# Output projection, cross-attention and feed-forward of a decoder layer merged into one program

## What is computed

```python
x = x + attn(layernorm(x), Wq, Wk, Wv, Wo)      # ends with ctx @ Wo.T
x = x + xattn(layernorm(x), ctx, ctx)           # 8 heads of 64 token rows per sequence
x = x + ffn(layernorm(x), w_gate, w_up, w_down)

def xattn(q, k, v):                             # q is the normed x, rows are tokens
    qh = q.reshape(b * 8, 64, 512); kh = k.reshape(b * 8, 64, 512); vh = v.reshape(b * 8, 64, 512)
    sm = softmax(einsum('bdm,bdn->bmn', qh, kh) / 8, axis=-1)
    return einsum('bmn,bcn->bcm', sm, vh).reshape(b, 512, 512)

def qlinear(x, w):                              # the feed-forward's three products
    wq, ws = round_clip(w / mean|w|); xq, xs = round_clip(x / (max|x| / 127))
    return (xq @ wq.T) * xs * ws
ffn = qlinear(silu(qlinear(x, w_gate)) * qlinear(x, w_up), w_down)
```

## Time and profile before

| | |
|---|---|
| median of three runs | 911.53 us (908.85 to 912.01) |
| the profiled execution | 906.05 us |
| its span, first to last instruction | 904.2 us |
| busy share of the span, PE / DVE / ACT / POOL | 87% / 77% / 50% / 45% |
| TensorE's mean granted clock | 0.958 of full speed |
| a and b, up to the last DVE instruction of b | 0 to 403.2 us |
| c, first transpose to last norm | 409.3 to 481.3 us |
| d, first to last compute | 487.6 to 713.2 us |
| e, from its first load to the end | 713.6 to 904.2 us |

### The profile page before, as it was taken

The page is one execution under the profiler, slowest core; times in us unless marked ns, Lnnn a source line. Parts: engine busy times, 40 slices in busy tenths (PEclk is TensorE's granted clock), DMA queues, the critical chain, the costliest instruction groups (busy, mean ns, idle before and its releaser), DMA issues. The chain is left out here.

```text
span 904.2 us, 14319 instructions
## 1 busy us (share of the span) xinstructions
PE 789.2 (87%) x4306; PEld 404.1 (45%) x4306; DVE 696.3 (77%) x1982; ACT 453.7 (50%) x791; POOL 410.4 (45%) x412
## 2 busy tenths in 40 slices
PE   2999589999999999977884899999998379999997
PEld 1888334444444444436662444434433034444443
DVE  7554489888888889814775899898986478989984
ACT  2566147666776767652222555445544134455442
POOL 1556399999940000001223576667666323433331
PEclk9999779999999999998996899999999789999999
DMA  7987545555523223116995555655552224445443
GB/s 265 345 285 250 184 130 169 153 168 147 145 58 85 71 72 81 40 32 217 315 326 192 146 152 158 177 154 158 159 165 80 72 51 94 106 113 112 126 99 94
DMA packets 137101, 134.46 MB, mean 149 GB/s; under 512 B 87232, under 2 KB 99136, under 8 KB 133952
## 3 DMA queue, kind: packets, MB, share of 16 engines
q1 hardware_dynamic: 111488, 104.18, 39.6%
q10 hardware_dynamic: 23808, 16.78, 6.6%
q0 software_dynamic: 1728, 12.58, 4.2%
HBM read 89.65 MB, written 33.03 MB: 136 GB/s over the span
## 5 line engine op out<-in xcount | busy, mean ns | idle before, releaser
L584 DVE CUSTOM_DVE_ANT_0 b_junk<-b_p,mask_qk 128x128 bf16<-128x128 f32 (+3 forms) x512 | 217.7, 483 | 34.6 <-PE b_p L609 34.3
L531 ACT ACTIVATE b_probs<-b_p 128x512 f32<-128x512 f32 (+1 forms) x352 | 176.7, 560 | 49.0 <-PE b_p L641 27.2
L609 PE MATMUL b_p<-b_ks,b_qs 96*128 96x128 bf16 (+3 forms) x512 | 127.5, 314 | 16.0 <-DMA b_ks<-k_parts 10.0
L971 ACT ACTIVATE d_probs<-d_p 128x512 f32<-128x512 f32 x128 | 74.3, 594 | 106.5 <-PE d_p L1077 106.5
L638 PE MATMUL b_p<-b_qs,b_ks 98*128 98x512 bf16 (+1 forms) x352 | 123.0, 364 | 2.8 <-DMA b_qs<-b_mrow 1.8
L944 POOL TENSOR_TENSOR d_halves<-d_probs 128x1024 f32<-128x1024 f32 x32 | 76.2, 2382 | 54.0 <-ACT d_probs L971 53.9
L730 POOL TENSOR_SCALAR c_veps<-c_mv 128x1 f32<-128x1 f32 x16 | 7.1, 446 | 204.2 <-DVE c_mv L779 204.2
L995 DVE TENSOR_REDUCE d_mx<-d_p 128x1 f32<-128x512 f32 x128 | 83.7, 670 | 18.6 <-PE d_p L1060 17.5
L1341 PE MATMUL e_pg<-wg,e_xt 128*128 128x512 bf16 x256 | 67.0, 385 | 18.7 <-DMA e_xt<-e_xq 18.7
L609 PEld LDWEIGHTS b_p<-b_ks,b_qs 96*128 96x128 bf16 x512 | 45.3, 100 | 81.5 <-DVE b_mx L584 19.5
L1060 PE MATMUL d_p<-d_kk,qh 128*128 128x512 f32 x128 | 62.3, 493 | 21.6 <-DVE d_kk L1010 12.4
(11 more groups left out here) (141 smaller groups left out, 1512.0 us busy)
## 6 DMA issues: line engine op xcount, KB each, us to landing
k<-in_ctx SPq DMA_DIRECT2D x64, 128.0 KB, 2.6
qh<-x_normed_high SPq DMA_DIRECT2D x64, 128.0 KB, 2.8
q_parts<-a_parts SPq DMA_DIRECT2D x16, 384.0 KB, 4.3
b_qs<-q_parts SPq DMA_DIRECT2D x32, 192.0 KB, 3.4
a_x<-in_x SPq DMA_DIRECT2D x4, 1024.0 KB, 5.6
a_wst<-in_w_gate SPq DMA_DIRECT2D x4, 1024.0 KB, 6.8
a_wst<-in_w_up SPq DMA_DIRECT2D x4, 1024.0 KB, 8.5
a_wst<-in_w_down SPq DMA_DIRECT2D x4, 1024.0 KB, 8.5
```

Source lines behind the costliest of these rows:

```text
L531: nc.scalar.activation(pblock(j % 2, kb)[:, j0:j0 + nj, c:c + w], p2[(NE * j + n) % BANKS2][:, 0:nj * w].rearrange("p (j c) -> p j c", j=n ...
L584: best = nc.vector.tensor_tensor_reduce(out=junk[:, 2 * ((NU * i + k) % BANKS1) + n, 0:w], in0=bank[:, c:c + w], in1=keep["mask_qk"][:, SE ...
L609: last = nc.tensor.matmul(p1_bank(i, k)[:, c:c + w], qs[0:STACK, s, j, qt * P:(qt + 1) * P], ks[0:STACK, s, 0:w], start=True, stop=True)
L971: nc.scalar.activation(probs[:, s3, n, :], p2[(KD * s3 + n) % BANKS][:], ACT.Exp, scale=SCALE).then_inc(exps, 1)
```

## The change

The last three programs become one, `rest_of_layer` (names r_ in the trace), in one block, after the same a and b. What it does:

- Self-attention writes its output straight into an SBUF tile `tok` (16 tiles of 128 tokens), instead of a staging tile that ACT's queue stored to DRAM. The output projection reads `tok`, adds x and writes back to `tok`; cross-attention adds to it; the feed-forward reads it. The DRAM tensors `attn_out`, `x1` and `x2` and their loads and stores are gone. The normed rows still go through DRAM.
- `in_turn` puts the three stages' steps into one order for every engine: the first four steps of cross-attention (0 to 3) stand behind the last four of the output projection; the feed-forward's steps 0 and 1 behind cross-attention's 31 and 33, and its steps 2 to 9 behind cross-attention's 35 to 42.
- The reciprocal is taken on the 16 by 64 distinct sums of a pair: ACT copies `pd` to `den`, ACT's queue brings one row of each head into `few` (two DMAs), DVE inverts it, SP's queue stores it to DRAM (one DMA) and loads it back spread over 64 partitions each (two DMAs, `rden`). ACT copies `pn` to `y`, and DVE multiplies `y` by `rden`, both in SBUF.
- PE does F and S of a step without a break, then `sum_probs` and two parts of `weigh` in even steps, the other two in odd ones, and each lags the scores by more steps.
- In the feed-forward's steps SP's queue turns `zq` (before: `xq`) ahead of `hq`, no longer behind it.

The core of the diff:

```diff
-                if 0 <= j4 < STEPS:
-                    s, g = j4 % BATCH, j4 // BATCH
-                    act.wait_ge(p1_used, USE[i, OUT] + 1)
-                    act.dma_start(scr["o"][SEQ * s:SEQ * (s + 1), bass.ds(HEADROWS * g, HEADROWS)].rearrange("(t p) c -> p t c", p=P),
-                                  o[:, s, :, :]).then_inc(o_out[s], 16)
...
-                        nc.vector.tensor_tensor(o[:, j % UNROLL, :, :].rearrange("p t (j d) -> p t j d", j=GSZ), turned[:, :, :, 0:HDIM],
+                        s, g = j % BATCH, j // BATCH
+                        nc.vector.tensor_tensor(tok[:, TPB * s:TPB * (s + 1), HEADROWS * g:HEADROWS * (g + 1)].rearrange("p t (j d) -> p t j d", j=GSZ), turned[:, :, :, 0:HDIM],
...
+        C_LAST, D_LAST, E_LAST = TILES + 3, HEADS_X + 11, TILES + 5
+        D_EARLY = 4
+        E_BESIDE = {HEADS_X - 1: 0, HEADS_X + 1: 1}
+        E_BESIDE.update({HEADS_X + 3 + k: 2 + k for k in range(D_LAST - HEADS_X - 3)})
+
+        def in_turn(attend_output, attend_context, feed):
+
+            for i in range(C_LAST):
+                attend_output(i)
+                if i >= C_LAST - D_EARLY:
+                    attend_context(i - (C_LAST - D_EARLY))
+            for i in range(D_EARLY, D_LAST):
+                attend_context(i)
+                if i in E_BESIDE:
+                    feed(E_BESIDE[i])
+            for i in range(len(E_BESIDE), E_LAST):
+                feed(i)
...
+        def pair_due(i, behind):
+
+            s = i - behind
+            return s // 2 if s >= 0 and s % 2 == 0 and s < HEADS_X else None
 
...
+                p = pair_due(i, 10)
+                if p is not None:
+                    sp.wait_ge(inv_done, p + 1)
+                    sp.dma_start(scr["inv"][2 * RUNS * p:2 * RUNS * (p + 1), :], inv[:, p % 2, :]).then_inc(inv_out, 16)
...
+                p = pair_due(i, 11)
+                if p is not None:
+                    sp.wait_ge(inv_out, 16 * (p + 1))
+                    if due(p):
+                        sp.wait_ge(y_done, p)
+                    for a in range(2):
+                        at = RUNS * (2 * p + a)
+                        sp.dma_start(rden[a * H:(a + 1) * H, :], scr["inv"][at:at + RUNS, :].rearrange("r c -> (r c)")
+                                     .unsqueeze(0).broadcast_to([H, DIM])).then_inc(rden_in, 16)
...
+                        sp.wait_ge(S["up"], NB * (j - 1))
...
                 if 0 <= j < TILES:
...
                         sp.dma_start_transpose(ht[:, j % 2, n * KF // 2:(n + 1) * KF // 2, :],
                                                hq[:, j % 2, n * FF // 2:(n + 1) * FF // 2]).then_inc(ht_in[j % 2], 16)
...
+                p = pair_due(i, 11)
+                if p is not None:
+                    pool.wait_ge(y_done, p + 1)
+                    nc.gpsimd.tensor_tensor(tok[:, p, :], y[:, p % 2, :], tok[:, p, :], ALU.add).then_inc(x2_done, 1)
...
+                p = pair_due(i, 8)
+                if p is not None:
+                    act.wait_ge(weighted, p + 1)
+                    if due(p - 1):
+                        act.wait_ge(x2_done, p - 1)
+                    nc.scalar.activation(y[:, p % 2, :], pn[:], ACT.Copy).then_inc(y_kept, 1)
+                p = pair_due(i, 7)
+                if p is not None:
+                    act.wait_ge(summed, p + 1)
+                    if due(p):
+                        act.wait_ge(few_in, 32 * p)
+                    nc.scalar.activation(den[:], pd[:], ACT.Copy).then_inc(den_kept, 1)
...
+                    nc.scalar.activation(kk[:, i % UNROLL, :], k2[:, i % 2, :], ACT.Copy).then_inc(kk_done, 1)
+                exponential(1)
+                if p is not None:
...
+                    for a in range(2):
+                        act.dma_start(few[a * RUNS:(a + 1) * RUNS, p % 2, :],
+                                      den[a * H:a * H + 1, :].rearrange("o (r c) -> o r c", r=RUNS)).then_inc(few_in, 16)
+                exponential(2)
...
+                p = pair_due(i, 8)
+                if p is not None:
...
+                        dve.wait_ge(inv_out, 16 * (p - 1))
+                    nc.vector.reciprocal(inv[:, p % 2, :], few[:, p % 2, :]).then_inc(inv_done, 1)
...
+                p = pair_due(i, 11)
+                if p is not None:
+                    dve.wait_ge(rden_in, 32 * (p + 1))
+                    dve.wait_ge(y_kept, p + 1)
+                    nc.vector.tensor_tensor(y[:, p % 2, :], y[:, p % 2, :], rden[:], ALU.mult).then_inc(y_done, 1)
...
+                first_half, second_half = pair_due(i, 6), pair_due(i, 7)
+                if first_half is not None:
+                    sum_probs(first_half)
+                    weigh(first_half, 0)
+                    weigh(first_half, 1)
+                if second_half is not None:
+                    weigh(second_half, 2)
+                    weigh(second_half, 3)
```

More of the change, by code:

```diff
@@ L1212, in gate, with feed @@
+            def feed(i):
                 def gate(n):
@@ L1324, in _, with attend_output @@
                     nc.vector.tensor_scalar(cd[:, j % UNROLL:j % UNROLL + 1], sh[:, c], keep["wscale"][:, 2:3], None, ALU.mult).then_inc(S["cd"], 1)
+            in_turn(attend_output, attend_context, feed)
         @block.tensor
         def _(pe):
-            for i in range(LAST):
+            def attend_output(i):
+                if i < TILES:
+                    if due(i - 1):
+                        pe.wait_ge(C["lo"], i - 1)
+                    for k in range(KD):
+                        last = nc.tensor.transpose(tr[i % 2][:, k, :], tok[:, i, k * P:(k + 1) * P], keep["ident"][:])
+                    last.then_inc(C["turned"], 1)
+                j = i - 1
+                if 0 <= j < TILES:
+                    pe.wait_ge(C["lo"], j + 1)
+                    if due(j - 1):
+                        pe.wait_ge(C["x1"], j - 1)
+                    n = 0
+                    for k in range(KD):
+                        for xp, wp in ((hi, "wo_hi"), (hi, "wo_lo"), (lo, "wo_hi")):
+                            last = nc.tensor.matmul(pj[j % 2][:], xp[:, j % 2, k, :], keep[wp][:, k, :], start=n == 0,
+                                                    stop=n == 3 * KD - 1)
+                            n += 1
+                    last.then_inc(C["projected"], 1)
@@ L1340, in gate_up @@
                         for k in range(KD):
[L1341 removed]
+                            last = nc.tensor.matmul(bank[g % BANKS][:], zt[:, j % 2, k, :], keep[w][:, k, n * 512:(n + 1) * 512],
                                                     start=k == 0, stop=k == KD - 1)
@@ L1352, in _ @@
                     for k in range(KF):
-                        last = nc.tensor.matmul(pd[j % 2][:], ht[:, j % 2, k, :], keep["wd"][:, k, :], start=k == 0, stop=k == KF - 1)
+                        last = nc.tensor.matmul(pf[j % 2][:], ht[:, j % 2, k, :], keep["wd"][:, k, :], start=k == 0, stop=k == KF - 1)
                     last.then_inc(S["down"], 1)
+            in_turn(attend_output, attend_context, feed)
 def decoder(nc, io, out):
```

790 lines of the change are left out of this document (329 added, 461 removed).

## The result

The changed kernel takes **858.4 us**, median of four runs (856.35 to 862.99), where the kernel before took 910.19 (908.38 to 912.01) beside it: a ratio of 0.9446, interval 0.941 to 0.9483. The forecast was 857, in a range of 848 to 879. The profiled execution took 858.61 us, span 856.5; the sum had forecast 851.5 for it. So the sum promised 7.1 us more than came. That the median was hit to 1.4 us is luck: the profiled execution of before lay 5.5 under its median, and this one lies on it.

The account below looks back on a forecast made before the run. PE and DVE were taken to bound cross-attention together, PE alone the feed-forward, with idle time at block borders. Five terms summed to -54.6 us: 911.5 to 857 us, range 848 to 879.

Parts of the forecast that it names:

- term 1: Self-attention into projection: block end waits for no store, first transposes for no load, starting at about 404; -5.3 us.
- term 2: Projection into cross-attention: last norm and first row of maxima come earlier, first second scores at about 484.5; -6.5 us.
- Term 3: Steady cross-attention: DVE loses four reciprocals a pair, PE makes fewer changes; 5.8 us a head, not 6.4; -23.2 us.
- term 4: Cross-attention into feed-forward: PE's list goes on, 8.5 us to the gate against 29.7, including 1.3 delay through ACT; -21.1 us.
- term 5: Feed-forward: last pair's weighing fills early waits, but late inverses delay DVE, adding 2; +1.5 us (-0.5 to +8).
- the prediction's own sign: At the borders: the prediction is wrong in kind if PE waits there for anything but work.
- B: Cross-attention keeps its pace, 12.8 us a pair, as SP's issues or ACT's list replace DVE; +17, 874 us; chance 0.11.
- C: Border to feed-forward overlaps badly, POOL's and ACT's lists holding back first rounded rows; up to 10 lost, 867 us; chance 0.10.
- E: Cross-attention: inverses arrive too late in every pair, delaying y, last maximum and PE's turn; +64, 921 us; chance 0.03.
- the slack of 1.2 us: Steady cross-attention, round trip of the inverses: they land at 3.3 us into DVE's odd step, y wants them at 4.5.
- A: Cross-attention: SBUF access shared with POOL lengthens DVE's y and kk to near 1.6 us; +15, 872 us; chance 0.16.

Follow-up runs that it names:

- both of SP's edits: Changed kernel with SP's part of the feed-forward's second step one cross-attention step later and the last four pairs' inverses sent in their store's step: 849.82 us.
- SP's part late: Changed kernel with only SP's part of the feed-forward's second step moved behind cross-attention's step 34, no longer 33: 856.79 us.
- the edit: Changed kernel with the last four pairs' inverses sent in the step of their store, ahead of the feed-forward's transpositions: 855.19 us.
- kernels with early inverses: Changed kernel with the last four pairs' inverses sent early: alone 855.19 us, with SP's feed-forward part later 849.82, with ACT's later too 849.35.

## Why the prediction was right, and where it was off

The terms against the profiled executions, each from the starts above:

| term | forecast | measured |
|---|---|---|
| 1, self-attention into the projection | -5.3 | -5.4 |
| 2, projection into cross-attention | -6.5 | -7.4 |
| 3, cross-attention | -23.2 | -21.5 |
| 4, cross-attention into the feed-forward | -21.1 | -21.5 |
| 5, the feed-forward | +1.5 | +8.1 |
| sum | -54.6 | -47.7 |

**Terms 1 and 2** went as worked out: first transposes at 404.38 for 404, first second scores at 483.50 for 484.5. But 1.5 of term 2's 7.4 us are not the border's: from the first low part to the last it took 62.5 us before, with PE's clock at 0.50 over the first tiles, and 61.0 here at 1.00. In the executions with a lower clock there the term is -5.8. No edit tested the stores and loads of term 1 apart; the row says only that nothing but the block's start is waited for.

**Term 3** is right in kind: with DVE's reciprocals back it is gone (199.8 against 198.5 before). Its size came out by luck, of two errors that nearly cancel. Without the stall cross-attention is 170.6 us (both of SP's edits), 4.7 under the 175.3 forecast. Of that, 14 x (11.6 - 11.41) = 2.7 is the steady pair. The sum took 11.4 for the least that PE needs and added 0.2 for waits; its DVE rows add up to 9.2 to 9.65 a pair and not to 9.3 to 9.8, and DVE took 9.4 (132.09 of 160 us). PE needed 10.78, since matmuls of 128 by 64 in a block of eight or twelve take less than two or three times the 1.01 of four; and DVE's list added 0.5 to 0.9. Most of the rest of the 4.7 lies in the pairs ahead of the first `y`, which ran at 10.8. And the stall of 6.35 came on top. The step that failed is term 4's "ACT must take the feed-forward's first rounded rows ... delays ... PE by 1.3": the delay through ACT is there (1.69 with SP's part late), but the same step's transposition in SP's list, ahead of the last row of maxima, costs five times that. For this seam I had followed ACT's list, and SP's only for the inverses of term 5. By the prediction's own sign, PE waiting at a border for anything but work, it was wrong in kind at this place.

**Term 4** was right at 8.2 for 8.5.

**Term 5** is the term that was mis-sized. Its direction was given, and the upper bound of +8 was reached. The inverses behind the transpositions, put at 2, cost 4.5 (removed by the edit). The rest is at the end. The last tile's down product waits 4.50 us for its turned rows and takes 5.26, at a mean granted clock of 0.68. Before it was

```profile
897.30 3.61 PE L1353 MATMUL e_pd<-wd,e_ht 128*128 128x512 bf16 x16 [2.43 <-DMA e_ht<-e_hq]
```

at full clock. That is 2.1 and 1.7 us more. In the kernels with early inverses it still waits 3.94, 4.08 and 3.92. The trace shows where the turned rows lose time: DVE waits 2.01 us (835.72) for ACT's second Silu of the last tile, and ACT was at the rounded rows of the tile ahead (832.96 to 835.11). Before, the wait at that place was 0.31 (885.26). No run tested it.

**The rivals.** B, ACT or SP as the bound, did not come: SP's part is not full in the steady stretch, but its order cost at the seam. C, a bad border, is what happened in part, by 6.35 of the 10 it allowed, through SP and not only through POOL and ACT. E, inverses late in every pair, did not come: they landed 2.7 to 4.0 us after the issue. But the slack of 1.2 us was not there. In three of the nine steady pairs `y` waited for them, at most 0.45 us, and nothing hid it: from the `y` ahead to these three passed 11.71, 11.59 and 11.67 us, to the six others 11.27 to 11.31. So E's mechanism is there, at 1.1 us in all. With both of SP's edits one such wait was 1.20 us, and PE's turn behind it came 12.45 us after the one ahead. The inverses held DVE from pair 12 on. A, the shared access: its mechanism is there, its price small. `y` and `kk` as lines alone (shortest/median/longest in ns):

```profile
L1083 DVE TENSOR_TENSOR r_y<-r_y,r_rden x16: 691/693/2121, 528.9 to 738.3; 128x512 f32<-128x512 f32 x16
...
L1076 DVE TENSOR_TENSOR r_kk<-r_k,r_kk x32: 689/1469/1665, 470.9 to 640.6; 64x512 fp32r<-64x512 f32 x32
```

The trace of the changed kernel agrees with the rule of the Trainium skill ("GPSIMD Engine Reference", section Specifications) on two SBUF inputs: `y` in SBUF can take three times as long. Its starts and ends look as if DVE waits for the end of POOL's instruction: the long `y` (651.08 to 653.20) ended 0.55 us after POOL's `halves` (650.25 to 652.65), and a `kk` from 543.48 to 545.13 ended 0.55 after the `halves` of 542.18 to 544.58. That is argued from the rows alone, and POOL's ends are rough in a profile. But 14 of the 16 took 0.69, and one 0.98, since in the steady part `y` stands where POOL is between two instructions. `kk` stands beside POOL's sums, and its middle value rose from 1.22 to 1.47. So the place in the step decides the price.

## What to carry to other kernels

When stages are merged so that their steps overlap, walk each queue's list at the seam, not only the compute engines': an early step's DMA that waits for a late product holds back the small urgent transfer behind it (here one row of maxima, 6.35 us of PE idle). An overlap gives back in both neighbours some of what it gains at the border; measure the stages on both sides, and expect single repairs to move the loss to the next place in the same queue until all are made (here 3.7 and 5.3 us alone, some 11 together). A loop bound by DVE can be relieved by taking redundant elements out, here worth 22.8 us in this order at the price of five small DMAs a pair, as long as their use lies some steps later. Once that is done, look at what stands ahead of the result that the next engine wants: here one operation of 0.69 us ahead of the last maximum still lengthens each pair. An order with `y` behind that maximum wasn't tried with the round trip.
